# Two-pass head shifted by a one-tensor VectorE form, and one Gelu of 4096 columns per group of four tiles

## The reference, cut to what matters

```python
q = (xn @ w_q.T)...                         # xn: batch-normalised input
sim = einsum('pbnhd,hkpd->pbnhk', q, keys)  # 2 x 8 heads x 32 scores per row
s, i = top_k(sim, 8)
all_scores = sx[..., :, None] + sy[..., None, :]
scores, pk = top_k(all_scores, 8)           # 8 best of the pair sums, per head
o = einsum('bnd,bnhkd->bnhk', inputs, key_in[idx])
o = gelu(o, approximate=False) * softmax(scores)
out = einsum('bnhk,bnhkd->bnd', o, key_out[idx])
```

## Time and profile before

| | |
|---|---|
| median of 3 runs | 1744.48 us |
| profiled execution | 1744.04 us, its span 1742.3 us |
| busy over the span | DVE 1565.0 (90%), PE 1468.5 (84%), ACT 1318.5 (76%), POOL 1273.1 (73%) |
| attention | until about 713 us |
| groups 1 to 14 of the feed-forward part | 62.2 to 62.3 us each |

### The profile page before, as it was taken

One profiled execution on the slowest core, in us unless ns is written; L12 is line 12 of the kernel. 1 busy time (PEld: TensorE's weight loads), 2 busy tenths in 40 slices (PEclk: granted clock), 3 DMA queues, 4 the chain that ended last, 5 costly groups with the idle time before them and its releaser, 6 DMA issues.

```text
span 1742.3 us, 33161 instructions
## 1 busy us (share of the span) xinstructions
PE 1468.5 (84%) x10688; PEld 1008.1 (58%) x10688; DVE 1565.0 (90%) x4616; ACT 1318.5 (76%) x1805; POOL 1273.1 (73%) x1547
## 2 busy tenths in 40 slices
PE   2799999999999998557888888888887888878877
PEld 2355555555555553345667666666666666666666
DVE  3899999999999983499999999999999999999997
ACT  1277666666666666458898998989889899898985
POOL 1065555665556556598989989899898998989982
PEclk9799999999999999789999999999999999999999
DMA  5444544445544531100000000000000000000000
GB/s 136 89 97 115 116 109 112 108 113 112 108 116 109 113 65 33 49 0 19 1 19 19 1 19 20 7 13 19 19 1 20 19 2 19 19 8 12 13 7 7
DMA packets 73630, 86.39 MB, mean 50 GB/s; under 512 B 9873, under 2 KB 63761, under 8 KB 68753
## 3 DMA queue, kind: packets, MB, share of 16 engines
q1 hardware_dynamic: 73456, 84.27, 20.4%
HBM read 58.30 MB, written 25.95 MB: 48 GB/s over the span
## 4 chain that ended last, share of the span: by engine, by line
ACT 17%; DVE 14%; POOL 11%; issue 10%; PE 5%; DMA 1%; DVEq 0%; SPq 0%; ACTq 0%
POOL SUM L795 11%; ACT E L922 8%; DVE W L1029 8%; PE WT L1100 3%; ACT L835 2%; ACT L834 2%; ACT W L884 2%; DVE SMALL L975 1%; DVE M8Y L958 1%; DVE NL L985 1%; ACT SUM L878 1%; PE MB L1039 1%; ACT GE L834 1%; ACT BNT L843 1%; PE E L1052 0%
## 5 line engine op out<-in xcount | busy, mean ns | idle before, releaser
L795 POOL TENSOR_TENSOR SUM<-SIM 128x1024 f32<-128x1024 f32 x480 | 900.9, 1914 | 94.1 <-DVE W L1029 90.8
L1100 PE MATMUL WT<-idf,W 128*128 128x128 f32 x4096 | 545.7, 283 | 109.4 <-DVE W L1029 67.3
L1100 PEld LDWEIGHTS WT<-idf,W 128*128 128x128 f32 x4096 | 475.1, 146 | 267.5 <-DVE W L1029 144.3
L1029 DVE SCALAR_TENSOR_TENSOR W<-SUM,SMALL,E 128x1024 f32<-128x1024 f32 x448 | 567.0, 1280 | 28.3 <-ACT E L922 28.2
L922 ACT ACTIVATE E<-SUM,NB 128x1024 f32<-128x1024 f32 x448 | 499.7, 1116 | 91.2 <-DVE NB L986 72.6
L261 POOL TENSOR_SCALAR_AFFINE_SELECT PT<-PT 128x128 f32<-128x128 f32 (+1 forms) x1024 | 337.1, 355 | 256.4 <-ACT PT L355 223.0
L414 DVE CUSTOM_DVE_ANT_0 SY<-SY,bandf 128x384 f32<-128x384 f32 x512 | 273.1, 573 | 0.0
L355 ACT ACTIVATE PT<-TX 128x512 f32<-128x512 f32 x256 | 153.0, 598 | 114.0 <-PE TX L542 113.9
L429 DVE TENSOR_REDUCE mx<-SX 128x2 f32<-128x512 f32 x256 | 174.3, 681 | 57.6 <-PE SX L524 57.5
L357 ACT ACTIVATE PT<-TY 128x768 f32<-128x768 f32 x256 | 207.5, 810 | 3.7
L570 PE MATMUL PV<-PT,V 128*32 128x384 f32 (+1 forms) x2048 | 166.5, 443 | 2.6 <-POOL PT L261 2.4
(11 more groups left out here) (116 smaller groups left out, 1916.7 us busy)
## 6 DMA issues: line engine op xcount, KB each, us to landing
K<-k_parts SPq DMA_DIRECT2D x96, 192.0 KB
Q<-q_parts SPq DMA_DIRECT2D x288, 64.0 KB
q_parts<-qp SPq DMA_DIRECT2D x16, 384.0 KB, 2.4
k_parts<-kp SPq DMA_DIRECT2D x16, 384.0 KB, 2.4
xin<-in_x SPq DMA_DIRECT2D x16, 256.0 KB, 3.2
xres<-in_x SPq DMA_DIRECT2D x16, 256.0 KB, 9.7
x<-X SPq DMA_DIRECT2D x16, 256.0 KB, 2.2
x2T<-X2T SPq DMA_DIRECT2D x16, 256.0 KB, 2.1
```

The lines of the kernel that those rows point to most:

```text
L795: return eng.tensor_tensor(SUM[(q * FH + h) % RING][:, :].rearrange("p (i j) -> p i j", i=NK), sx, sy, ALU.add)
L1029: nc.vector.scalar_tensor_tensor(out=W[h % WRING][:, :], in0=SUM[(k * FH + h) % RING][:, :], scalar=TOP[q][:, h, TOPK - 1:TOPK], in1=E[(n ...
L1100: o = pe.matmul(WT[:, e, :], W[h % WRING][:, e * P:(e + 1) * P], ident[:, :], is_transpose=True, start=(h == 0 and e % 4 == 0), stop=(h == ...
```

## The change

Three edits.

1. NL, one column, is computed by `tensor_scalar` with the tile's eighth best as pointer scalar, (LZ - D) * -1, in place of a `tensor_tensor` D - LZ of two SBUF tensors. The value is the same.
2. `gelus` runs once in a group, on all 4096 columns of GE, at (k, h) = (0, 3). It waits for all 8 expert copies, and DVE's wait for it is one count a group in place of two.
3. The parts get three tables. In tile k = 0, at h = 4, DVE searches all of tile 1 and ranks all of tile 2 (16 more MAX8 than tile 1 alone; before, 8). Tile 1 only does tile 2's parts 4 and 5, with the two-pass head's pair sum of tile 2 at h = 2 and 3. Tiles 2 and 3 run the search of one tile ahead spread over h = 2, 3 and 4. SUMS_AHEAD becomes (0, 1): DVE sums the two-pass head of tiles 1 and 2, before of 1 and 3.

```diff
-SUMS_AHEAD = (0, 2)
-EVEN_PARTS = ((), (), (), (), ((1, 0), (1, 1), (1, 2), (1, 3), (1, 4), (1, 5), (1, 8), (2, 0), (2, 1), (1, 9)), (), ((1, 6),), ((1, 7),))
-ODD_PARTS = ((), (), ((1, 2),), ((1, 3),), ((1, 4), (1, 5)), (), ((1, 6),), ((1, 7),))
+SUMS_AHEAD = (0, 1)
+GAP_PARTS = ((), (), (), (), ((1, 0), (1, 1), (1, 2), (1, 3), (1, 4), (1, 5), (1, 8), (2, 0), (2, 1), (2, 2), (2, 3), (1, 9)), (), ((1, 6),), ((1, 7),))
+LATER_PARTS = ((), (), ((1, 8),), ((1, 9),), ((1, 4), (1, 5)), (), ((1, 6),), ((1, 7),))
+NORMAL_PARTS = ((), (), ((1, 0), (1, 1)), ((1, 2), (1, 3)), ((1, 4), (1, 5)), (), ((1, 6),), ((1, 7),))
+PARTS = (GAP_PARTS, LATER_PARTS, NORMAL_PARTS, NORMAL_PARTS)
...
-        def gelus(g, b, half):
-            act.wait_ge(S["expert_copied"], g * BLK + (half + 1) * 4)
-            o = GE[b][:, 4 * half:4 * half + 4, :].rearrange("p e n -> p (e n)")
+        def gelus(g, b):
+            act.wait_ge(S["expert_copied"], (g + 1) * BLK)
+            o = GE[b][:, :, :].rearrange("p e n -> p (e n)")
...
-                    if (k, h) == (2, 3) and more:
-                        gelus(g + 1, 1 - b, 0)
                     if (k, h) == (0, 3) and real:
-                        gelus(g, b, 1)
+                        gelus(g, b)
...
-                nc.vector.tensor_tensor(NL[q][:, :], D8[:, LH, TOPK - 1:TOPK], LZ[:, LH:LH + 1], ALU.subtract)
+                nc.vector.tensor_scalar(NL[q][:, :], LZ[:, LH:LH + 1], D8[:, LH, TOPK - 1:TOPK], -1.0, ALU.subtract, ALU.mult)
...
-            dve.wait_ge(S["gelu_ready"], (g + 1) * 2)
+            dve.wait_ge(S["gelu_ready"], g + 1)
...
-                    for ahead, part in (ODD_PARTS if k % 2 else EVEN_PARTS)[h]:
+                    for ahead, part in PARTS[k][h]:
```

More of the change, by code:

```diff
@@ L857, in _ @@
         act.wait_ge(S["expert_copied"], BLK)
-        act.sem_inc(S["gelu_ready"], 2)
+        act.sem_inc(S["gelu_ready"], 1)
         nc.scalar.preload_act_table_set("natural_log_exp_and_others")
```

## The result

The changed kernel takes 1694.11 us (median of 4 runs, 1691.62 to 1698.76) against 1744.54 for the kernel before (1743.83 to 1745.17): a ratio of 0.971, 95% interval 0.969 to 0.974. That is faster. It is 15 us more than the 1679 forecast and inside the range of 1653 to 1703. The profiled execution took 1693.73 us, its span is 1692.0.

The account below looks back on a forecast made before the run. DVE's chain was taken as the bound. Groups 1 to 14 save 14 x 3.2 = 45, group 0 19, group 15 1: 65 off a span of 1742.3, plus 1.74, gives 1679 us; range 1653 to 1703 (8 in 10).

Parts of the forecast that it names:

- What bounds the kernel, and NL: DVE's own chain, 60.56 us a group, bounds; the new NL takes 1.28 a tile, 5.1 a group, off it.
- The reason given against the second port: At NL: te, a tensor_scalar within SBUF on 4 columns, takes 169 ns without a spread of POOL's size.
- the third rival: NL still waits for POOL by its port, whatever the instruction: group 62.75, 1751 us; chance 6%.
- The Gelu and the gap: Tile 0: one Gelu of 3.67 us, DVE idle 1.5 once, PE waits 4.4, tile takes 18.0.
- Worth nothing by itself: The merged Gelu: ACT loses 2.57 of table loads and 0.16 a group, but ACT is not the bound.
- Tiles 1 to 3: Mask 7 waits 0.3 to 0.4 for E of head 7; tile 1 takes 13.6, tiles 2 and 3 13.45 each.
- PE behind the gap: After PE's idle time the low clock makes CT wait 0.5 to 0.6 for PE; 0.55 charged in every group.
- the second rival: PE takes DVE's place: low clock outlasts the gap's tail, CT 2.5 to 3 late; group 61.3, 1711 us; 16%.
- Sum: The whole group: 58.5 us from the tiles plus 0.55 for PE's clock, 59.05, a saving of 3.2.
- POOL didn't become the bound: First rival: POOL, with 56.2 us of sums, bounds a group of some 56.7; time 1646 us; 14%.
- PE in DVE's place: The second rival: CT 2.5 to 3 us late once a group behind the gap; 1711 us; 16%.
- if the long waits became frequent it would be worse: Condition on the third rival's 1751 us, which assumes the one long NL wait in group 0 stays.

Follow-up runs that it names:

- e1: The kernel before with only the NL line changed (two Gelus and old parts stay): 1690.16 us, ratio 0.966 to the kernel before.
- e3: The changed kernel plus 32 transposes of zeros on PE in the gap of tile 0: 1684.7 us, ratio 0.963 to the kernel before.
- e6: e1 with NL's tensor_scalar over 8 columns, one of them used: 1746.52 us, one timed run.
- e10: e1 with NL's tensor_scalar over 2 columns, one of them used: 1744.96 us, one timed run.
- e11: e1 with NL's tensor_scalar over 3 columns, one of them used: 1745.65 us, one timed run.
- e2: The changed kernel with the old NL line put back (merged Gelu and new parts stay): 1786.63 us, ratio 1.022 to the kernel before.

## Why the prediction was right, and where it was off

- **What bounds the kernel, and NL.** Right: DVE's chain fell by about 5 us a group with NL. The cost taken was 0.07 from NL to NB; it is 0.12 to 0.13 (1087.64 to 1087.76). The reason given against the second port was not sound. te's 169 ns at 4 columns was read as showing that a `tensor_scalar` within SBUF doesn't wait, but NL at 2, 3 and 8 columns does. te's own row has a greatest value of 316 ns, and the trace says what it is. POOL works in SBUF on PT there, in instructions of 0.29 and 0.41 us. Fourteen of the 16 te begin with only 0.06 us of one of them left (once 0.13) and take 169 to 172 ns, one meets none, and the one that begins with 0.29 us left waits to its end, 691.16:

```profile
690.39 0.77 POOL L261 TENSOR_SCALAR_AFFINE_SELECT PT<-PT 128x256 f32<-128x256 f32 x2 [0.15 <-ACT PT L357]
690.86 0.32 DVE L393 TENSOR_SCALAR te<-tv 128x4 f32<-128x4 f32 x1
```

So te had hardly met POOL, and its spread was of the size of POOL's instructions there. The edit escaped by its single column, which the prediction named ("at one column") without a row for it. A chance of 6% for the third rival was too small for what the rows could bear.
- **The Gelu and the gap.** Right in size: 3.62 for 3.67, a wait of 1.50 for 1.5, tile 0 17.95 for 18.0, PE's idle time 4.08 for 4.4. "Worth nothing by itself" was too kind: e1 shows that it costs 0.45 a group, which the sum had no term for, as it never set the new NL against the old gaps.
- **Tiles 1 to 3.** Mask 7 waits 0.37 to 0.39, as forecast. Tiles 2 and 3 take 13.65 for 13.45, tile 1 without PE's lateness 13.7 for 13.6: half a microsecond a group too little, 7 us in 14 groups.
- **PE behind the gap.** The mechanism was right, the term too small: 0.55 charged. CT's waits are 0.32 to 0.42 and 1.38 to 1.52 in turn, 0.93 on average. Part of that only takes the place of a later wait (mask 2 waits 0.15 behind BNT here, 0.35 in e3), so tile 1 is 0.74 longer than in e3 (14.47 for 13.73): 0.19 a group too little, 3 us in 14 groups. What was missed is that the low clock can outlast SIM and slow the transposes as well, which only the second rival had.
- **Sum.** 59.05 forecast, 59.72 measured: 9 us of the 15 that are missing, 7 from tiles 1 to 3 and 3 from PE, less 1 from tile 0. Group 0 gave 1.4 less, and the attention part's 4.4 are of no mechanism that the forecast treats.
- **The rivals.** POOL didn't become the bound: from group 4 on it idles 2.5 to 4.1 us a group. PE in DVE's place happened in a small part: CT is up to 1.5 us late in every other group, where the rival had 2.5 to 3 in each. The third rival is what e6, e10 and e11 are, at 1745 to 1747 us against 1751 forecast, but with the old gaps; with the merged gap it costs 1787, since "if the long waits became frequent it would be worse" came true (e2).

## What to carry to other kernels

A one-element instruction of 1.4 us is a queue, not work: look for another engine's instruction that ends when it does, and then change which memory or how many columns it reads. Test each edit of a pair alone; here one brought all of the gain, and the other took some back and would have been a loss of 2.2% without it. Where an engine must wait through a gap, count what the gap does to TensorE behind it, and leave the idle engine something harmless to do.

## What the runs showed of the hardware that was not expected

- `tensor_scalar` from SBUF to SBUF waits for POOL's `tensor_tensor` at 2, 3 and 8 columns (medians 1440, 1439, 1442 ns) and not at one (208 ns, greatest 216 in e1). `tensor_tensor` of one column with one input in PSUM doesn't wait (151). `tensor_scalar` of 4 columns waits in the same way for POOL's instructions on PT, the one time that it meets one with 0.29 us left (316 ns for 169).
- How long such an instruction waits depends on more than the running sum: it ended at the next boundary (1.43 us), or at the end of POOL's whole run (15.37 for 8 more sums, 3.84 in e2). What decides between the two stays open; it wasn't tried. The moment within the sum alone doesn't: in group 0 of the kernel before, one NL began 1.51 us into a sum and took 0.42, the next began 1.48 into one and took 15.37.
- The same 4.08 us of idle time in PE was followed by a low clock that covered SIM and little else in one of the groups shown, and the next 16 transposes too in the other; over groups 1 to 14 CT's waits of 0.3 to 0.4 and of 1.4 to 1.5 us alternate strictly. 3.7 us of transposes of zeros removed both.
